# Half-batch maxima and a split mask in the first layer of a two-layer transformer kernel

## The chip, the core and the metric

One core of a Trainium2 chip. A core has TensorE (matrix products, its weight loads are shown as PEld), VectorE (DVE), ScalarE (ACT), GpSimd (POOL) and SyncE (SP, which here only issues DMAs); they meet through semaphores. The metric is the time of the whole program in microseconds on the device, where lower is better. Three runs of the kernel before gave 719.17, 721.73 and 725.0 us (median 721.73).

## The reference

Four batches of 512 tokens with 128 channels go through: a feed-forward block (ternary weights, gelu), the attention that this case is about, a second such feed-forward block, a routed block of 8 experts, a linear attention and a second routed block. The attention of the first layer has 16 heads of 8 channels and two halves. The first is a causal softmax attention whose values are the normalised input; the second, the error attention, applies masked products to what the first one failed to predict:

```python
scores = jnp.einsum('bhqd,bhkd->bhqk', q, k) * scale
scores = jnp.where(causal, scores, -jnp.inf)
y_ar = jnp.einsum('bhqk,bhkd->bhqd', jax.nn.softmax(scores, axis=-1), v)
e = v[:, :, 1:, :] - y_ar[:, :, :-1, :]
qa = -jax.nn.leaky_relu(-q2 * scale, negative_slope=0.02)
ka = jax.nn.sigmoid(k2 * scale * 0.02)
ma = jnp.einsum('bhqd,bhkd->bhqk', qa, ka)
ma = jnp.where(jnp.tril(jnp.ones((t - 1, t - 1), dtype=bool)), ma, 0.0)
y_ma = jnp.einsum('bhqk,bhkd->bhqd', ma, e)
```

## The kernel before

Tokens lie in 4 tiles of 128, heads in 4 sets of 4. A softmax needs the largest score of every query and head before the exponentials. The kernel computes the scores twice for that: once with queries on the partitions, for the **maxima**, and once with keys on the partitions, for the exponentials; the negated maxima are an additional row of the operands of the second product, so that ScalarE's exponential needs nothing more.

**Maxima.** One unit of them is a product of a query tile with a key tile of one set (128x512, on the diagonal with a second product that adds the mask) into one of two PSUM banks (turn[1] and accum[1], in turns), and VectorE's reduction of it to 128x4 (L1059, tile sb_mpart). There are 10 units to a set and 40 to a batch. `max_scores` (L1486) issues the products on TensorE, `maxima` (L1055) the reductions. After all 40, VectorE takes the largest over the tiles (`max_of_tiles`, L1063), TensorE turns the result around into turn[1] (`max_turn`, L1500), ScalarE copies it to SBUF (`max_t`, L788, tile sb_qs), and two small DMAs to a pair of sets put it into the operands (`max_row`, L398). The operands of the maxima come from DRAM, one set at a time (`next_max_set`, L390: 5 DMAs, issued when the products of the set two before are done).

**Before the attention** there is one `before_attention(b)` per batch on every engine: the feed-forward block's output product, the hidden product of the next batch, the turns and the projections of batch b-1 (`project`). Projections are split in a high and a low part and stored in DRAM (`keep_softmax`, `keep_features` on SP: 6 DMAs of 256 KB each for a batch). All 40 units of batch 0 are done here: 12 in `before_attention(2)`, 12 in `before_attention(3)` and 16 behind it. They can't start before the operands of batch 0 have been to DRAM and back.

**The attention of a batch** is a loop of 20 units of exponentials (5 to a set). In unit u TensorE issues the scores of unit u+2, the first of two maxima units of the next batch, the products with the values (`answers`, in the second, fourth and fifth unit of a set only), at the second unit of a set the turn of the answers of the set before, and the second maxima unit. ScalarE takes a unit's exponential (L812); TensorE's scores of unit u+2 wait for the exponential of unit u. At the first unit of a set ScalarE also copies the answers of the set before out of PSUM (L803). Batch 3 has no next batch, so its loop has no maxima. The operands of the exponentials are two sets deep; SP loads the set two further on when the scores of a set are through, behind the maxima's set in its queue.

**The error attention** of the batch follows. For each of 4 key tiles TensorE makes two products of 128x1024 (`ma_scores`, pair[0] and pair[1]), VectorE masks both to SBUF (L1132, tile sb_work) and masks a 128x128 state (L1137), and TensorE multiplies with the errors (`ma_answers`). The errors are GpSimd's (`errors`, L615: L624 and L625), the last of them for the last set of heads, and TensorE waits for them before the first product.

Each engine executes its own list in the order in which the Python code issues it; there is no planner. A wait thus holds back everything that stands behind it on its engine.

## Time and profile before

| | |
|---|---|
| runs | 719.17, 721.73, 725.0 us |
| profiled execution | 721.84 us, of which the span is 720.0 us |
| TensorE busy | 511.9 us (71%) |
| VectorE busy | 365.3 us (51%) |
| ScalarE busy | 196.8 us (27%) |
| GpSimd busy | 182.3 us (25%) |
| mean granted TensorE clock | 0.863 of 2.4 GHz |
| attention of the four batches | from 128.5 to 364 us |

The page's chain that ended last is by share: PE 47%, DVE 18%, POOL 11%, issue 8%, DMA 6%, ACT 5%, SP's queue 5%. Busy times are averages over stages that have different limits, so what counts is read stage by stage.

### The profile page before, as it was taken

What the parts mean: (1) busy time and instruction counts of PE and PEld (TensorE: products, weight loads), DVE (VectorE), ACT (ScalarE), POOL (GpSimd) and SP (SyncE); (2) the same over time, 40 slices, a digit from 0 to 9 for tenths busy, and PEclk for the clock granted to TensorE, in tenths of its full rate; (3) what the DMA queues carried; (4) which work ended last, traced back from release to release, by engine and by line L of the source; (5) the groups of instructions that cost most, each with busy time, mean ns of one, the idle gap of its engine ahead of it and who ended that gap; (6) DMA issues with size and microseconds to landing.
All of it is one profiled execution on the core that took longest, in us unless ns stands there. A gap on an engine that the chain in (4) does not pass through costs nothing.

```text
span 720.0 us, 9924 instructions
## 1 busy us (share of the span) xinstructions
PE 511.9 (71%) x3706; PEld 329.5 (46%) x3706; DVE 365.3 (51%) x950; ACT 196.8 (27%) x278; POOL 182.3 (25%) x208
## 2 busy tenths in 40 slices
PE   1755784799899889998878529914778888735930
PEld 1624432344634544453467517802445655524930
DVE  4444745367676856760535431224969677430211
ACT  1342231453245144336234302102223111101200
POOL 8550436001010110111012560045322022031035
PEclk9987887699999999999989958965899999655975
DMA  8434668732442253142070012114743530001213
GB/s 282 185 116 148 210 212 248 177 103 64 92 133 78 79 131 104 53 90 82 1 234 1 30 39 57 45 32 132 203 142 79 160 97 16 1 15 51 60 40 98
DMA packets 61471, 74.16 MB, mean 103 GB/s; under 512 B 6772, under 2 KB 38128, under 8 KB 61168
## 3 DMA queue, kind: packets, MB, share of 16 engines
q1 hardware_dynamic: 59376, 69.34, 33.3%
q0 software_dynamic: 2048, 4.20, 2.0%
q8 instruction: 29, 0.48, 0.3%
q14 instruction: 18, 0.15, 0.1%
HBM read 42.97 MB, written 30.41 MB: 102 GB/s over the span
## 4 chain that ended last, share of the span: by engine, by line
PE 47%; DVE 18%; POOL 11%; issue 8%; DMA 6%; ACT 5%; SPq 5%; POOLq 0%; DVEq 0%; ACTq 0%
PE ps_accum L1378 21%; PE ps_pair L1378 16%; PE ps_turn L1378 5%; POOL xe_scr L574 4%; DMA sb_ring<-sb_qs 3%; SPq L358 2%; POOL sb_rstd L558 2%; PE ps_turn L1386 2%; DVE sb_work L1132 2%; POOL sb_work L720 2%; DVE sb_work L1270 1%; DVE sb_mpart L1059 1%; DVE sb_values L969 1%; DVE sb_stats L960 1%; SPq L366 1%
## 5 line engine op out<-in xcount | busy, mean ns | idle before, releaser
L812 ACT ACTIVATE sb_work<-ps_pair 128x1024 f32<-128x1024 f32 x80 | 80.3, 1026 | 51.0 <-PE ps_pair L1378 50.2
L1059 DVE TENSOR_REDUCE sb_mpart<-ps_turn 128x4 f32<-128x512 f32 x80 | 55.0, 687 | 46.6 <-PE ps_turn L1378 46.5
L1378 PE MATMUL ps_pair<-sb_ring,sb_xsets 128*128 128x512 f32 x160 | 64.5, 480 | 15.6 <-DMA sb_ring<-sb_qs 10.1
L1059 DVE TENSOR_REDUCE sb_mpart<-ps_accum 128x4 f32<-128x512 f32 x80 | 55.0, 688 | 20.9 <-PE ps_accum L1378 20.2
L1378 PE MATMUL ps_accum<-sb_work,sb_v_aug 128*32 128x128 f32 (+3 forms) x768 | 58.6, 400 | 0.3 <-ACT sb_work L812 0.3
L1378 PE MATMUL ps_turn<-sb_ring,sb_m_sets 128*128 128x512 f32 x80 | 40.5, 506 | 20.7 <-DMA sb_m_sets<-q_scr 11.0
L1378 PE MATMUL ps_accum<-sb_ring,sb_m_sets 128*128 128x512 f32 x80 | 42.0, 525 | 3.9 <-DVE sb_mpart L1059 3.7
L1378 PEld LDWEIGHTS ps_pair<-sb_ring,sb_xsets 128*128 128x128 f32 x160 | 30.7, 199 | 26.6 <-issue 14.5
L556 POOL TENSOR_SCALAR sb_ve<-sb_mv 128x4 f32<-128x4 f32 x24 | 5.6, 235 | 144.4 <-DVE sb_mv L963 144.0
L624 POOL TENSOR_TENSOR sb_e_pad<-sb_v_next,sb_y_ar 128x128 f32<-128x128 f32 x16 | 7.3, 458 | 127.2 <-DVE sb_y_ar L1102 127.2
L1270 DVE TENSOR_TENSOR sb_work<-ps_pair,sb_cst 128x1024 f32<-128x1024 f32 x32 | 37.5, 1215 | 2.2 <-PE ps_pair L1378 2.2
L1132 DVE TENSOR_TENSOR sb_work<-ps_pair,sb_cst 128x1024 f32<-128x1024 f32 x32 | 37.7, 1218 | 1.1 <-PE ps_pair L1378 0.4
L1378 PE MATMUL ps_pair<-sb_y_tmp,sb_mw 128*128 128x256 f32 x128 | 34.9, 421 | 1.9 <-ACT sb_y_tmp L862 1.9
L1386 PE MATMUL ps_turn<-sb_cst,sb_values 128*128 128x128 f32 x48 | 10.3, 354 | 34.1 <-DVE sb_values L969 29.7
L574 POOL DMA_INDIRECT xe_scr<-sb_values,sb_slot_all x16 | 15.9, 997 | 73.3 <-DVE sb_slot_all L1040 69.7
L1378 PE MATMUL ps_pair<-sb_xs,sb_w1r 128*128 128x512 f32 x64 | 23.7, 496 | 13.7 <-DVE sb_xs L979 7.1
L1378 PE MATMUL ps_accum<-sb_mw,sb_work 128*128 128x128 f32 x256 | 31.3, 276 | 2.3 <-issue 2.3
L1378 PEld LDWEIGHTS ps_accum<-sb_mw,sb_work 128*128 128x128 f32 x256 | 30.0, 192 | 2.7 <-issue 2.6
L1378 PEld LDWEIGHTS ps_turn<-sb_ring,sb_m_sets 128*128 128x128 f32 x80 | 16.1, 201 | 30.7 <-DVE sb_mpart L1059 12.6
L1217 DVE COPY sb_e_pad<-ps_accum 128x256 f32<-128x256 f32 x16 | 6.8, 425 | 45.4 <-PE ps_accum L1378 45.4
L1378 PE MATMUL ps_pair<-sb_ring,sb_ka_stk 128*128 128x512 f32 x64 | 23.9, 483 | 7.9 <-DVE sb_work L1270 6.5
L1378 PEld LDWEIGHTS ps_pair<-sb_y_tmp,sb_mw 128*128 128x128 f32 x128 | 25.8, 212 | 7.0 <-ACT sb_y_tmp L862 3.5
(242 smaller groups left out, 1007.7 us busy)
## 6 DMA issues: line engine op xcount, KB each, us to landing
sb_m_sets<-q_scr SPq DMA_DIRECT2D x16, 256.0 KB
sb_xsets<-k_scr SPq DMA_DIRECT2D x16, 256.0 KB
sb_ka_stk<-mk_scr SPq DMA_DIRECT2D x4, 1024.0 KB
sb_mw<-in_mw SPq DMA_DIRECT2D x16, 256.0 KB, 5.2
sb_ka_stk<-mk_scr SPq DMA_DIRECT2D x8, 512.0 KB
q_scr<-sb_qs SPq DMA_DIRECT2D x12, 256.0 KB, 3.0
k_scr<-sb_ks SPq DMA_DIRECT2D x12, 256.0 KB, 3.8
sb_ring<-k_scr SPq DMA_DIRECT2D x64, 48.0 KB
```

Source lines behind the costliest of these rows:

```text
L358: sp.dma_start(ring[VW * hl:VW * hl + 3 * HD, i, hl].bitcast(F32), head_rows(q_scr, b, HL * hs + hl, 3 * HD)).then_inc(done, 16)
L366: sp.dma_start(ring[VW * hl:VW * hl + 3 * HD, 2 + i, hl].bitcast(F32), head_rows(k_scr, b, HL * hs + hl, 3 * HD)).then_inc(done, 16)
L558: pool.tensor_tensor(rstd[i][:], ve[i][:], const("minus_half"), ALU.pow).then_inc(s["rstd"], 1)
L574: pool.indirect_dma_start(xe_scr, bass.IndirectOffsetOnAxis(ap=places[:, t:t + 1], axis=0), rows_out[:, t, :], None).then_inc(s["scattered ...
L624: pool.tensor_tensor(dst, value, answer, ALU.subtract).then_inc(s["err_pad"], 1)
L720: pool.indirect_dma_start(y_last[:, b, t, :], None, ye_scr, bass.IndirectOffsetOnAxis(ap=slot_all[:, i:i + 1], axis=0)).then_inc(last_gath ...
L812: act.activation(banks[:, 2 * i:2 * i + 2], pair[u % 2][:], ACT.Exp, scale=SCALE).then_inc(s["exp_done"], 1)
L1059: dve.tensor_reduce(mpart[:, m // NPAIR, m % NPAIR, :], max_banks[m % 2][:].rearrange("p (h k) -> p h k", h=HL), AX.X, ALU.max).then_inc(s ...
L1132: dve.tensor_tensor(work[:, n % 4].rearrange("p a (h q) -> p (a h) q", h=HL), pair[n % 2][:].rearrange("p a (h q) -> p (a h) q", h=HL), bc ...
L1270: dve.tensor_tensor(work[:, n % 4].rearrange("p a (h q) -> p (a h) q", h=HL), pair[n % 2][:].rearrange("p a (h q) -> p (a h) q", h=HL), bc ...
L1378: return pe.matmul(dst, lhsT, rhs, start=start, stop=stop, skip_group_check=True)
L1386: last = pe.transpose(tile(dst, t), src[:, t, :], ident)
```

## The change

Two things change. The maxima of a batch are made in two halves (two sets, 20 units, each) with a turn of their own, and all of them come half a batch later. Before the attention only the first half of batch 0 is made, 12 units of it in `before_attention(3)` and 8 behind. The second half of batch 0 is made in the first five units of its own attention, four maxima units in each. From there on a set of maxima (10 units) goes with each set of exponentials: the loop of batch b makes the maxima's set that is three sets ahead, so that the first five units of batch 3 have maxima too. The turns of the halves now lie inside the loop, at the first unit of the second and of the fourth set. And of the two masks of each key tile of the error attention, VectorE keeps the first; the second is a copy by ScalarE and a select in place by GpSimd.

```diff
+def max_units(b, u):
+    hs, i = u // NG_X, u % NG_X
+    if b == 0 and hs == 0:
+        return HALF + 4 * i, HALF + 4 * i + 2, HALF + 4 * i + 4
+    first = NPAIR * (NS * b + NS - 1 + hs)
+    if first >= UNITS:
+        return UNITS, UNITS, UNITS
+    at = (0, 0, 3, 5, 8, 10) if hs % 2 else (0, 2, 4, 6, 8, 10)
+    return first + at[i], first + (at[i] + at[i + 1]) // 2, first + at[i + 1]
+
+
+def max_turn_in(b, u):
+    if u == NG_X:
+        return 2 * b + 1
+    if u == 3 * NG_X and b + 1 < B:
+        return 2 * b + 2
+    return None
 
 
 def build(nc, x_in, bias_cols, w_attn_t, w_k2_t, w_proj_t, b_proj, w1_t, w2_t, b2,
@@ -213,7 +234,7 @@
...
             keep_softmax(2)
+            next_max_set(0)
             keep_features(2)
+            next_max_set(1)
             keep_softmax(3)
+            keep_features(3)
             hold(sp, s["ffn_h"], NF * B)
...
-            keep_features(3)
...
-            next_max_set(0, 2)
             hold(sp, s["max_t_evac"], 1)
...
-            next_max_set(0, 3)
-            for kept in ("mq_kept", "mk_kept"):
+            for kept in ("q_kept", "k_kept", "mq_kept", "mk_kept"):
                 hold(sp, s[kept], 48 * B)
...
             for b in range(B):
+                if b == 0:
+                    next_max_set(2)
                 load_state(b)
...
                 for hs in range(NS):
-                    if b + 1 < B:
-                        next_max_set(b + 1, hs)
+                    if NS * b + NS - 1 + hs < B * NS:
+                        next_max_set(NS * b + NS - 1 + hs)
                     hold(sp, s["st_mm"], NX * b + NG_X * (hs + 1))
                     if hs + 2 < NS:
                         load_exp_set(b, hs + 2)
+                        hold(sp, s["max_t_evac"], 2 * b + 2)
                         max_row(b, hs + 2)
                     elif b + 1 < B:
                         load_exp_set(b + 1, hs + 2 - NS)
-                if b + 1 < B:
-                    hold(sp, s["max_t_evac"], b + 2)
-                    for hs in range(2):
-                        max_row(b + 1, hs)
+                        hold(sp, s["max_t_evac"], 2 * b + 3)
+                        max_row(b + 1, hs + 2 - NS)
...
+            def zero_from(b, t):
+
+                block = work[:, (2 * t + 1) % 4].rearrange("p a (h q) -> p (a h) q", h=HL)
+                pool.wait_ge(s["ma_copied"], NT * b + t + 1)
+                pool.affine_select(block, block, [[0, 2 * HL], [1, P]], ALU.is_ge, 0.0, base=-1,
+                                   channel_multiplier=-1).then_inc(s["ma_zeroed"], 1)
+
...
                 for hs in range(NS - 1):
                     errors(b, hs)
+                zero_from(b, 0)
+                errors(b, NS - 1)
+                for t in range(1, NT):
+                    zero_from(b, t)
                 if b + 1 < B:
                     values(b + 1)
-                errors(b, NS - 1)
...
+                act.copy(mT[q % 2], turn[1][0:H // 2, :]).then_inc(s["max_t_evac"], 1)
...
                         answers_out(b, hs - 1)
+                    if max_turn_in(b, u) is not None:
+                        max_t(max_turn_in(b, u))
                 answers_out(b, NS - 1)
-                if b + 1 < B:
-                    max_t(b + 1)
+                for t in range(NT):
+                    act.wait_ge(s["ma_mm"], 2 * NT * b + 2 * t + 2)
+                    if t >= 2:
+                        act.wait_ge(s["ym_mm"], NT * b + t - 1)
+                    act.copy(work[:, (2 * t + 1) % 4], pair[1][:]).then_inc(s["ma_copied"], 1)
...
             def attention(b):
...
+                for u in range(NX):
+                    hs, i = u // NG_X, u % NG_X
+                    first, _, last = max_units(b, u)
+                    maxima(first, last)
+                    if b and u == 1:
                         moments(norm_first(B + b - 1), x[b - 1], (b - 1) % 2)
-                    maxima(b + 1, 4, 6)
-                    if b:
+                    if b and u == 2:
                         normalise(norm_first(B + b - 1), x[b - 1], xn_third[b - 1], (b - 1) % 2)
-                    for hs in range(NS):
-                        maxima(b + 1, at[hs], at[hs + 1])
-                        if hs < NS - 1:
-                            answers_divide(b, hs)
-                    max_of_tiles(b + 1)
-                else:
-                    norm(norm_first(B + b - 1), x[b - 1], xn_third[b - 1])
-                    for hs in range(NS - 1):
-                        answers_divide(b, hs)
+                    if u + 1 < NX and max_turn_in(b, u + 1) is not None:
+                        max_of_tiles(max_turn_in(b, u + 1))
+                    if hs and i == 1:
...
-                for n in range(2 * NT):
+                for t in range(NT):
+                    n = 2 * t
                     dve.wait_ge(s["ma_mm"], 2 * NT * b + n + 1)
                     if n >= 4:
                         dve.wait_ge(s["ym_mm"], NT * b + (n - 4) // 2 + 1)
                     dve.tensor_tensor(work[:, n % 4].rearrange("p a (h q) -> p (a h) q", h=HL),
-                                      pair[n % 2][:].rearrange("p a (h q) -> p (a h) q", h=HL),
+                                      pair[0][:].rearrange("p a (h q) -> p (a h) q", h=HL),
                                       bc(const("key_before"), 2 * HL), ALU.mult).then_inc(s["ma_masked"], 1)
-                    if n % 2 == 1 and n // 2 < NT - 1:
-                        dve.wait_ge(s["kv_mm"], (NT - 1) * b + n // 2 + 1)
-                        dve.tensor_tensor(kv[:, n // 2, :], turn[0][:, 0:D], const("same_head"), ALU.mult).then_inc(s["kv_evac"], 1)
...
-                m = 3 * NT * (b - 2)
-                output(b, (lambda i: max_scores(0, m + i, m + i + 1)) if b >= 2 else None)
-                if b + 1 < B:
-                    hidden(b + 1, (lambda i: max_scores(0, m + 4 + i, m + 5 + i)) if b >= 2 else None)
+                last = b == B - 1
+                output(b, (lambda i: max_scores(i, i + 1)) if last else None)
+                if last:
+                    max_scores(4, 8)
                 else:
-                    max_scores(0, m + 4, m + 8)
+                    hidden(b + 1)
                 if b >= 2:
                     turn_keys(b - 2)
...
-                if b >= 2:
-                    max_scores(0, m + 8, m + 12)
+                if last:
+                    max_scores(8, 12)
...
+                    q, j = n // HALF, n % HALF
+                    if n % NPAIR == 0:
+                        pe.wait_ge(s[f"mset{hs % 2}"], 80 * (n // NPAIR // 2 + 1))
+                    if j >= 2:
+                        pe.wait_ge(s["smax_red"], (HALF + NT) * q + j - 1)
+                    elif j == 0 and q:
+                        pe.wait_ge(s["max_t_evac"], q)
...
+            def max_turn(q):
+                half = q % 2
+                pe.wait_ge(s["smax_red"], (HALF + NT) * (q + 1))
...
-                    if n >= 2:
-                        pe.wait_ge(s["ma_masked"], 2 * NT * b + n - 1)
+                    if t:
+                        pe.wait_ge((s["ma_masked"], s["ma_copied"])[pr], NT * b + t)
...
-                pe.wait_ge(s["ma_masked"], 2 * NT * b + 2 * t + 2)
+                pe.wait_ge(s["ma_masked"], NT * b + t + 1)
+                pe.wait_ge(s["ma_zeroed"], NT * b + t + 1)
...
                     if u + 2 < NX:
                         scores(b, u + 2)
-                    if ahead:
-                        max_scores(b + 1, 2 * u, 2 * u + 1)
+                    first, middle, last = max_units(b, u)
+                    max_scores(first, middle)
                     for kt in range(NT):
                         if (DIAGONAL[kt] + NT - kt - 1) // 2 == i:
                             answers(b, hs, kt)
                     if hs and i == 1:
                         turn_answers(b, hs - 1)
-                    if ahead:
-                        max_scores(b + 1, 2 * u + 1, 2 * u + 2)
+                    if max_turn_in(b, u) is not None:
+                        max_turn(max_turn_in(b, u))
+                    max_scores(middle, last)
 
                 pe.wait_ge(s["exp_done"], NX * (b + 1))
                 pe.wait_ge(s["state_in"], 112 * b + 112)
                 ma_scores(b, 0)
                 turn_answers(b, NS - 1)
-                if ahead:
...
                 if ahead:
-                    pe.wait_ge(s["max_t_evac"], b + 2)
+                    pe.wait_ge(s["smax_red"], (HALF + NT) * (2 * b + 3) + NPAIR)
```

How this moves instructions, at three places. The first is ScalarE's list in the attention of batch 0 at the start of the fourth set (ACTIVATE is the exponential, COPY the answers, CAST the turned maxima). Before:

```order
L812 ACTIVATE sb_work<-ps_pair1 128x1024 [waits s_pv_mm,s_st_mm]
L803 COPY sb_y_tmp0<-ps_accum0 128x512 [waits s_y_t,s_pv_mm]
L812 ACTIVATE sb_work<-ps_pair0 128x1024 [waits s_pv_mm,s_st_mm]
L812 ACTIVATE sb_work<-ps_pair1 128x1024 [waits s_pv_mm,s_st_mm]
L812 ACTIVATE sb_work<-ps_pair0 128x1024 [waits s_pv_mm,s_st_mm]
```

and with the change:

```order
L838 ACTIVATE sb_work<-ps_pair1 128x1024 [waits s_pv_mm,s_st_mm]
L829 COPY sb_y_tmp0<-ps_accum0 128x512 [waits s_y_t,s_pv_mm]
L822 CAST sb_qs<-ps_turn1 8x512 [waits s_xset1,s_xset0,s_max_t]
L838 ACTIVATE sb_work<-ps_pair0 128x1024 [waits s_pv_mm,s_st_mm]
L838 ACTIVATE sb_work<-ps_pair1 128x1024 [waits s_pv_mm,s_st_mm]
L838 ACTIVATE sb_work<-ps_pair0 128x1024 [waits s_pv_mm,s_st_mm]
```

The CAST stands now between two exponentials; before it stood behind the last COPY of the batch, outside the loop.

The second is GpSimd's list at the end of the attention of batch 0 (the two TENSOR_TENSOR are the errors of a set, COPY the values of the next batch). Before:

```order
L624 TENSOR_TENSOR sb_e_pad<-sb_v_next,sb_y_ar 128x4x4x8 [waits s_y_norm]
L625 TENSOR_TENSOR sb_v_next<-sb_v_next,sb_y_ar 128x4x32
L612 COPY sb_v_aug<-sb_values_1 128x64x8 [waits s_v_in,s_pv_mm]
L624 TENSOR_TENSOR sb_e_pad<-sb_v_next,sb_y_ar 128x4x4x8 [waits s_y_norm]
L625 TENSOR_TENSOR sb_v_next<-sb_v_next,sb_y_ar 128x4x32
L556 TENSOR_SCALAR sb_ve_0<-sb_mv_0 128x4 [waits s_moments]
```

and with the change:

```order
L640 TENSOR_TENSOR sb_e_pad<-sb_v_next,sb_y_ar 128x4x4x8 [waits s_y_norm]
L641 TENSOR_TENSOR sb_v_next<-sb_v_next,sb_y_ar 128x4x32
L647 AFFINE_SELECT sb_work<-sb_work 128x1024 [waits s_ma_copied]
L640 TENSOR_TENSOR sb_e_pad<-sb_v_next,sb_y_ar 128x4x4x8 [waits s_y_norm]
L641 TENSOR_TENSOR sb_v_next<-sb_v_next,sb_y_ar 128x4x32
L647 AFFINE_SELECT sb_work<-sb_work 128x1024 [waits s_ma_copied] x3
L628 COPY sb_v_aug<-sb_values_1 128x64x8 [waits s_v_in,s_pv_mm]
```

A select stands ahead of the errors of the last set, three behind them, and the values of the next batch behind all.

The third is SP's list before the attention, from batch 2's features on (mq_scr, mk_scr) over batch 3's stores to the operands of the exponentials (sb_xsets). Before:

```order
L352 DMA mq_scr<-sb_feat 16x8x512 [waits s_ma_lo]
L352 DMA mq_scr<-sb_feat 16x8x512 x2
L352 DMA mk_scr<-sb_feat 16x8x512 [waits s_ma_lo]
L352 DMA mk_scr<-sb_feat 16x8x512 x2
L352 DMA q_scr<-sb_qs 16x8x512 [waits s_split_lo]
L352 DMA q_scr<-sb_qs 16x8x512 x2
L352 DMA k_scr<-sb_ks 16x8x512 [waits s_split_lo]
L352 DMA k_scr<-sb_ks 16x8x512 x2
L358 DMA sb_ring<-q_scr 24x512 [waits s_ffn_h]
L358 DMA sb_ring<-q_scr 24x512 x3
L360 DMA sb_xsets<-k_scr 128x512
L358 DMA sb_ring<-q_scr 24x512 x4
```

and with the change, from batch 2's features on:

```order
L373 DMA mq_scr<-sb_feat 16x8x512 [waits s_ma_lo]
L373 DMA mq_scr<-sb_feat 16x8x512 x2
L373 DMA mk_scr<-sb_feat 16x8x512 [waits s_ma_lo]
L373 DMA mk_scr<-sb_feat 16x8x512 x2
L387 DMA sb_ring<-k_scr 24x512 [waits s_smax_mm]
L387 DMA sb_ring<-k_scr 24x512 x3
L389 DMA sb_m_sets<-q_scr 128x512
L373 DMA q_scr<-sb_qs 16x8x512 [waits s_split_lo]
L373 DMA q_scr<-sb_qs 16x8x512 x2
L373 DMA k_scr<-sb_ks 16x8x512 [waits s_split_lo]
L373 DMA k_scr<-sb_ks 16x8x512 x2
L373 DMA mq_scr<-sb_feat 16x8x512 [waits s_ma_lo]
L373 DMA mq_scr<-sb_feat 16x8x512 x2
```

A set of maxima with its wait (s_smax_mm) now stands ahead of the stores of batch 3.

## Rows read from the trace of the kernel before

**Rows 1.** Stretches from the span's start; busy time and count by engine, clock, DMA.

```profile
48.00:59.00 11.00, 0.07 (x1) 0.07 (x1) 0.79 (x2) 1.78 (x4) 4.89 (x4) 0.68 0.64 196
...
195.00:257.00 62.00, 56.37 (x430) 29.57 (x428) 43.18 (x78) 23.43 (x27) 6.64 (x12) 1.00 0.39 101
```

**Rows 2.** Timeline, TensorE before the attention: start, duration, instruction, idle before and releaser.

```profile
58.93 0.80 PE L1378 MATMUL ps_turn<-sb_ring,sb_m_sets 128*128 128x512 f32 x1 [11.02 <-DMA sb_m_sets<-q_scr]
...
71.87 1.98 PE L1378 MATMUL ps_pair<-sb_xnT,sb_wqk 128*128 128x512 f32 x4 [0.68 <-ACT sb_xnT L734]
...
78.09 1.05 PE L1378 MATMUL ps_accum<-sb_w,sb_h_too 128*128 128x128 f32 x8
...
91.75 3.78 PE L1378 MATMUL ps_pair<-sb_xnT,sb_wqk 128*128 128x512 f32 x4 [0.68 <-ACT sb_xnT L734]
...
104.72 1.98 PE L1378 MATMUL ps_pair<-sb_xnT,sb_wqk 128*128 128x512 f32 x4
```

**Rows 3.** Timeline, the queue of SP and what ends beside it, 108 to 129.

```profile
108.84 1.81 SPq L352 DMA_DIRECT2D q_scr<-sb_qs  x3
...
112.25 0.68 DVE L1059 TENSOR_REDUCE sb_mpart<-ps_accum 128x4 f32<-128x512 f32 x1
...
125.41 1.36 SPq L400 DMA_DIRECT2D sb_ring<-sb_qs  x2
...
128.49 0.76 PE L1378 MATMUL ps_pair<-sb_ring,sb_xsets 128*128 128x512 f32 x1 [7.78 <-DMA sb_ring<-sb_qs]
```

**Rows 4.** Timeline, the turn of the maxima: last reduction and ScalarE's copy.

```profile
118.65 0.69 DVE L1059 TENSOR_REDUCE sb_mpart<-ps_accum 128x4 f32<-128x512 f32 x1 [0.23 <-PE ps_accum L1378]
...
120.75 0.57 ACT L796 CAST sb_qs<-ps_turn 16x512 fp32r<-16x512 f32 x1 [7.24 <-PE ps_turn L1503]
```

**Rows 5.** Timeline, batch 1, border between two sets of heads.

```profile
207.51 1.95 ACT L812 ACTIVATE sb_work<-ps_pair 128x1024 f32<-128x1024 f32 x2
...
207.67 0.69 DVE L1059 TENSOR_REDUCE sb_mpart<-ps_accum 128x4 f32<-128x512 f32 x1 [0.76 <-PE ps_accum L1378]
...
208.85 0.63 PE L1378 MATMUL ps_pair<-sb_ring,sb_xsets 128*128 128x512 f32 x2
```

**Rows 6.** Timeline, VectorE's reciprocals: one per set, batches 1 and 3.

```profile
211.92 0.26 DVE L1100 RECIPROCAL sb_rcp<-ps_turn 128x16 f32<-128x16 f32 x1 [0.89 <-PE ps_turn L1538]
...
223.15 0.26 DVE L1100 RECIPROCAL sb_rcp<-ps_turn 128x16 f32<-128x16 f32 x1 [0.89 <-PE ps_turn L1538]
...
338.24 0.26 DVE L1100 RECIPROCAL sb_rcp<-ps_turn 128x16 f32<-128x16 f32 x1 [7.97 <-PE ps_turn L1538]
...
346.03 0.26 DVE L1100 RECIPROCAL sb_rcp<-ps_turn 128x16 f32<-128x16 f32 x1 [7.20 <-PE ps_turn L1538]
```

**Rows 7.** Timeline, SP's queue in batch 0.

```profile
132.28 7.68 SPq L388 DMA_DIRECT2D sb_values<-v_scr  x1
...
149.04 0.60 SPq L400 DMA_DIRECT2D sb_ring<-sb_qs  x1
```

**Rows 8.** Timeline, batch 3, first border between sets.

```profile
325.55 0.59 ACT L803 COPY sb_y_tmp<-ps_accum 128x512 f32<-128x512 f32 x1 [1.02 <-PE ps_accum L1378]
...
330.78 0.49 PE L1378 MATMUL ps_pair<-sb_ring,sb_xsets 128*128 128x512 f32 x1 [0.44 <-DMA sb_ring<-sb_qs]
```

**Rows 9.** Groups by line and form: the masks, and GpSimd's elementwise instructions.

```profile
L1132 DVE TENSOR_TENSOR sb_work<-ps_pair,sb_cst 128x1024 f32<-128x1024 f32 x32 | 37.7, 1218 | 1.1 <-PE ps_pair L1378 0.4
...
L612 POOL COPY sb_v_aug<-sb_values 128x512 f32<-128x512 f32 x4 | 2.4, 612 | 16.8 <-PE ps_accum L1378 10.0 <-DMA sb_values<-v_scr 6.8
...
L683 POOL TENSOR_TENSOR sb_x<-sb_x,sb_rows 128x512 f32<-128x512 f32 x4 | 5.1, 1272 | 3.3 <-DVE sb_values L969 3.2
...
L642 POOL TENSOR_SCALAR sb_rows<-sb_rows 128x128 f32<-128x128 f32 x1 | 1.0, 1013 | 2.4 <-DMA sb_l1wp<-in_l_wp 2.4
```

**Rows 10.** Timeline, TensorE takes up the error attention of batch 0.

```profile
179.99 0.46 PE L1378 MATMUL ps_turn<-sb_v_next,sb_ka_tok 128*128 128x128 f32 x2 [1.06 <-POOL sb_v_next L625]
```

**Rows 11.** Waits of TensorE, 197 to 241: us in total, times, longest.

```profile
PE ps_turn L1378 <- DVE sb_mpart L1059: 1.0, 2, 0.5
```

115 lines of the change are left out of this document (53 added, 62 removed).

## The prediction

> **What bounds the kernel now.** I read the busy time by stretch first, to see which stage has idle TensorE time; then TensorE's timeline before the attention, for what it waits for; then SP's queue, because it ends that stage; then the loop of the attention at a border of two sets, where the new turns go; and the groups of masks and of GpSimd's instructions for the second part of the change.
>
> Before the attention TensorE stands still from 48 to 59 (0.07 us busy) [rows 1]: the first maxima product starts at 58.93 after 11.02 us of waiting for batch 0's operands to come back from DRAM [rows 2]. From there projections of batches 1, 2 and 3 start at 71.87, 91.75 and 104.72 [rows 2]. Behind the last, SP is the path: stores of batch 3 from 108.84, the row of maxima at 125.41, first scores at 128.49 [rows 3]. In the loop TensorE is the bound: its waits for reductions are 1.0 us of 44 us [rows 11], and a set takes 223.15 - 211.92 = 11.2 us with ten maxima units against 346.03 - 338.24 = 7.8 us without [rows 6]. One maxima unit so costs (11.2 - 7.8) / 10 = 0.34 us of the path there. The error attention is VectorE's: 8 masks of 1.22 us per batch [rows 9].
>
> **Start of the attention: 13.3 us earlier.** The stall goes, since before_attention(2) has no maxima left. From 58.93 to 71.87 are 12.9 us with 8 maxima units; without them 12.9 - 8 x 0.34 = 10.2, and these now start at 47.9: projection 1 at 58.1. From there to projection 2 were 19.9 us; the four units between them and the output product at 78.09 go, so that this product starts right behind the projection's three products, some 3.1 us after their start (the first two take 1.98), instead of 6.2 [rows 2]: projection 2 at 74.9. The next interval keeps its maxima and its 13.0 us: projection 3 at 87.9, 16.8 us earlier. What is late next is SP: the stores of batch 3 started 4.1 us after the projection, but now a set of maxima with a wait for the 20th unit stands ahead. Its counterpart in place (the second unit after the projection) was reduced at 112.25, 7.5 us after it [rows 3]. That delays the chain by 3.4 us, so 16.8 - 3.4 = 13.4; the DMAs in the chain are otherwise the same, one set's load merely changes place. Bounds: -10 if saturated DMA engines delay the stores by one more wait, -18 if TensorE runs these stretches at the full clock and SP's list drains faster. I take -13.4.
>
> **The maxima moved into loops: +8.8 us.** Ten more units lie in batch 0's first five exponentials, and ten in batch 3's. Batch 0: 10 x 0.34 = 3.4, and part of them at the lower clock with which that loop starts: 4.5. Batch 3: here I follow the end instead. Its first border is set by the copy at 325.55 and ends with the scores at 330.78 that wait for a DMA [rows 8]. With 3.4 us more ahead, the last reduction falls at about 329.3; the turn chain below puts the next exponentials at 332.0, three of them follow, and the scores start at 335.1: +4.3. SP's list gives the same, as it now waits for the last maxima before it loads the set.
>
> **The turns: +17.4 us.** This is the term that decides. Before, the turn lay behind the loop, beside other work. Now the chain stands between two exponentials: last reduction, reduction over the tiles, four transposes, ScalarE's copy, and only then the exponential that TensorE's next scores need. Its length is in the trace: reduction at 118.65, copy at 120.75 for 0.57, so the next exponential starts 2.7 us after the last reduction starts [rows 4]. At a border in batch 1 the reduction starts at 207.67 and the exponential had started at 207.51 already, the scores that need it at 208.85 [rows 5]. Now: exponential at 207.67 + 2.7 = 210.4, over at 211.4, scores at 211.4 instead of 208.85, 2.55 us later. TensorE has nothing else in that unit: the two maxima units that stood there (0.68 us) have gone to later units of the set and are still to be done. The 0.3 us wait for a DMA some units later is absorbed. 2.55 + 0.68 - 0.3 = 2.9 us a turn. There are two turns in each of batches 0 to 2 (batch 3's is in the term above): 6 x 2.9 = 17.4. From both sides: 0.6 us (the transposes alone, if the rest hides) to 3.2.
>
> **SP in batch 0: +2 us.** The set ahead of the error attention's operands now waits for the 30th unit, in the third unit of the loop. Behind it stands the load that held the queue 7.68 us [rows 7], and behind that the exponentials' set that was complete after 149.04. I estimate this set some 30 us after the loop's start, about when the loop, with its extra maxima and its turn, comes to it: 0 to 5, taken 2.
>
> **The error attention: -2 us.** VectorE's list falls from two masks a tile to one: 4 x 1.22 less per batch, 19.5 us of VectorE in all. But the second half now passes ScalarE (two exponentials of that size take 1.95 us [rows 5]) and then GpSimd before TensorE may use it. No row shows a select. Below: the one-input COPY of 128x512 takes 612 ns, so 128x1024 some 1.1 us; above: the two-input form of 128x512 takes 1272 ns, so 2.5 us; farther, TENSOR_SCALAR takes 1.0 us for only 128 columns [rows 9], which would be 7 us. I take 1.5 us, between the first two and nearer to the one-input row, as a select reads one tensor. TensorE started behind the errors at 179.99 [rows 10]; one select stands ahead of these now, so it starts 1.5 us later. Then a tile takes about 2.2 us instead of 2.6: 3 x 0.4 are won, and 0.7 more at the end, where a second mask of 1.22 fell away. That is -0.5 a batch. At 1.1 us it is -1.3, at 2.5 us select follows select, and it is +2.5. So -2, with -5 and +10.
>
> The page "GPSIMD Engine Reference" of the Trainium skill (section 7) puts bodies of compare and select at 1.03 to 2.03 cycles for an element. With its 1.2 GHz that would be an estimate of 0.9 to 1.7 us for 1024, and the term -6 to +1. Its section 4.1 advises against elementwise work there but for one-input forms; here the COPY row agrees.
>
> **Sum.** -13.4 + 4.5 + 4.3 + 17.4 + 2 - 2 = +12.8, on the profiled execution's 721.84: 734.6 us. That execution stands 0.1 above the median of 721.73. I predict **734 us**. About 1% (7 us) is what a measurement of this kernel tells from no change.
>
> **Rivals.**
> 1. *The turn is covered; faster.* If the engines absorb it (TensorE gets ahead elsewhere, for instance since fewer maxima lie next to ScalarE's copy of the answers), a turn costs its 0.6 us of transposes: 6 x 2.3 = 13.8 less, and with DVE waits of 1.8 us a batch gone (rows 11 has 1.0 of them) 5 less: 734 - 19 = 715. It decides below 1 us a turn. For it: each engine's share in the loop leaves ScalarE free over half of the time. Against: the scores need exactly the exponential behind the turn, and no row shows a spare 2.5 us. 0.11.
> 2. *The start gains all that it can.* Projections at the full clock and DMAs never late would bring the loop's start forward by 24 us (the 11.0 stall, 12 units' waits before projection 2 and 3): 734 - 10 = 724, no change. Against: the stores' chain of 16.6 us behind projection 3 stays. Together with mixtures of small terms: 0.17.
> 3. *The select is slow.* At 2.35 us or more GpSimd is the bound of the error attention: 734 + 10 = 744. At 7 us it would be far more (+65). 0.14, of which 0.02 for the last.
> 4. *The clock falls.* Granted clock was 0.68 over the stretch with the 11 us pause, 1.00 over 195 to 257 with pauses of about 1 us [rows 1]. Idle times of 2.5 us lie between. If each turn cost the engine the full clock for half of the set behind it, 5.6 us of work take twice as long, and six turns add 6 x 5.6 = 34: 768. 0.06. The page "TensorE: Matmul & The Clock Gate" of the Trainium skill (Part 1) says that the lower clock is the default and recent activity lifts it; the two stretches agree with that (0.68 and 1.00), and neither tells what 2.5 us do.
>
> **Numbers.** The forecast has 0.52. Range 719 to 748: the forecast's own is 726 to 743 (start -10 to -18, turns 2.4 to 3.2, select 1.1 to 2); it is widened to rivals 2 and 3 without the 7 us case, and leaves out most of 1 and 4. Slower by over 1%: 0.52 + 0.14 + 0.06 less 0.02 for the forecast's lower edge, 0.70. Within 1%: 0.17 and half of that edge, 0.18. Faster by over 1%: 0.11 and the other half, 0.12.
>
> **What would show it.** First maxima product about 15 us after the second output product and no pause of 11 us; the first exponential scores at 115 instead of 128.5. In the loop the CAST between two exponentials, with TensorE idle about 2.5 us before the scores behind it, 7 times. A set of ten maxima with a turn at about 14 us instead of 11.2. The select at 1 to 2.5 us; error attention from the first product to the last at or a little below 15 us. Batch 0's loop longer by some 12 us, batches 1 and 2 by 6, batch 3 by 4. The prediction fails if a turn shows less than 1 us of idle TensorE, or if the start comes before 108 or after 120.

## The result

The changed kernel takes 759.25 us (median of 4 runs, 754.39 to 762.43), the kernel before beside it 721.23 us (median of 4 runs, 719.17 to 725.0). The ratio is 1.0515, with a 95% interval of 1.0443 to 1.0587: slower, as forecast, but by 38 us instead of 13, and outside the range of 719 to 748. The profiled execution, the longest of the four, has a span of 760.6 us against 720.0, so 40.6 us have to be found in the trace.

**The start** came as forecast. TensorE's timeline of the changed kernel has the projections of batches 1, 2 and 3 and then the first scores of the attention (start, duration, instruction, idle before and what ended it):

```profile
57.20 3.42 PE L1407 MATMUL ps_pair<-sb_xnT,sb_wqk 128*128 128x512 f32 x4 [0.68 <-ACT sb_xnT L760]
...
74.54 3.78 PE L1407 MATMUL ps_pair<-sb_xnT,sb_wqk 128*128 128x512 f32 x4 [0.68 <-ACT sb_xnT L760]
...
88.10 1.98 PE L1407 MATMUL ps_pair<-sb_xnT,sb_wqk 128*128 128x512 f32 x4 [0.21 <-ACT sb_xnT L760]
...
115.53 0.77 PE L1407 MATMUL ps_pair<-sb_ring,sb_xsets 128*128 128x512 f32 x1 [17.74 <-DMA sb_ring<-sb_qs]
```

Against [rows 2, 3] the loop starts at 115.53 instead of 128.49: 12.96 us won. All that is lost comes behind. To find it, the attention is cut at ScalarE's copies of the answers (one per set of heads) and at its last copy in the error attention; the first set of batch 0 is counted from the loop's first scores. The stretches of the kernel before that matter, in the view of busy time by stretch (length, then busy time and count of PE, PEld, DVE, ACT, POOL, then granted clock, DMA share, GB/s): the second and the fourth set of batch 1, its error attention, the first set of batch 3.

```profile
207.03:218.25 11.22, 10.68 (x65) 5.11 (x65) 7.27 (x12) 5.50 (x6) 0.87 (x2) 1.00 0.29 83
...
229.65:239.37 9.72, 9.48 (x60) 4.41 (x60) 6.92 (x12) 4.48 (x5) 0.87 (x2) 1.00 0.34 96
239.37:253.86 14.49, 12.72 (x171) 9.00 (x171) 11.87 (x19) 1.16 (x2) 1.48 (x3) 1.00 0.22 66
...
315.54:325.55 10.01, 8.81 (x60) 4.07 (x59) 3.75 (x14) 6.51 (x8) 2.55 (x3) 1.00 0.92 204
```

The same view of the changed kernel: the second set of batch 0; the second, third and fourth set of batch 1 and its error attention; the fourth set of batch 2; the first and second set of batch 3.

```profile
136.62:155.34 18.72, 13.49 (x70) 5.87 (x70) 8.12 (x17) 6.06 (x8) 0.87 (x2) 0.91 0.56 143
...
211.86:225.82 13.96, 11.71 (x69) 5.14 (x69) 7.52 (x16) 6.06 (x7) 0.87 (x2) 1.00 0.21 66
225.82:241.55 15.73, 13.36 (x65) 6.16 (x65) 7.19 (x12) 5.50 (x6) 0.86 (x2) 0.78 0.22 60
241.55:255.50 13.95, 10.52 (x64) 4.44 (x64) 7.52 (x16) 5.03 (x6) 0.86 (x2) 1.00 0.21 66
255.50:272.13 16.63, 13.20 (x167) 10.10 (x167) 7.02 (x10) 4.64 (x5) 5.77 (x7) 0.90 0.20 58
...
311.88:327.42 15.54, 12.13 (x64) 4.71 (x64) 7.53 (x16) 5.03 (x6) 0.87 (x2) 0.89 0.20 60
...
344.04:358.80 14.76, 12.44 (x72) 5.96 (x71) 9.39 (x23) 6.74 (x8) 2.54 (x3) 1.00 0.65 144
358.80:370.67 11.87, 9.72 (x57) 4.00 (x57) 1.68 (x7) 5.95 (x8) 0.87 (x2) 0.86 0.23 63
```

Two things are to be seen. A set with a turn is longer even where the clock stands at 1.00 (13.96 against 11.22, 13.95 against 9.72). And of stretches with the same work some have a lower clock and are some 1.6 us longer: the fourth set is 13.95 in batch 1 and 15.54 in batch 2. Set by set the differences to the kernel before are:

| | set 1 | set 2 | set 3 | set 4 | error attention | sum |
|---|---|---|---|---|---|---|
| batch 0 | +5.3 | +7.7 | -0.1 | +4.2 | +0.7 | +17.8 |
| batch 1 | 0.0 | +2.7 | +4.3 | +4.2 | +2.1 | +13.5 |
| batch 2 | 0.0 | +2.5 | -0.2 | +5.8 | +2.1 | +10.2 |
| batch 3 | +4.8 | +3.4 | 0.0 | 0.0 | +0.5 | +8.6 |

That is 50.1 us, less the 13.0 of the start: 37.1. The remaining 3.5 us (360.7 us against 357.2 from the last copy to the end) lie in code that the change doesn't touch. The profiles of the eleven experiments below, all with the same code there, have 355.6 to 364.4 us for it, so 3.5 us lie within its spread. Stages are compared below for that reason, beside the medians.

**A turn** is the chain that was forecast. Batch 1, border to the fourth set, all engines: last reduction, reduction over the tiles, transposes, ScalarE's copy, exponential, scores.

```profile
242.18 0.69 DVE L1090 TENSOR_REDUCE sb_mpart<-ps_accum 128x4 f32<-128x512 f32 x1 [1.12 <-PE ps_accum L1407]
...
243.40 0.60 PE L1537 MATMUL ps_turn<-sb_cst,sb_mneg 128*8 128x128 f32 x4 [0.57 <-DVE sb_mneg L1100]
244.03 0.57 ACT L822 CAST sb_qs<-ps_turn 8x512 fp32r<-8x512 f32 x1 [1.89 <-PE ps_turn L1537]
244.52 3.08 ACT L838 ACTIVATE sb_work<-ps_pair 128x1024 f32<-128x1024 f32 x3
245.58 0.73 PE L1407 MATMUL ps_pair<-sb_ring,sb_xsets 128*128 128x512 f32 x2 [1.58 <-ACT sb_work L838]
...
251.42 0.51 PE L1407 MATMUL ps_accum<-sb_ring,sb_m_sets 128*128 128x512 f32 x1 [0.72 <-DVE sb_mpart L1090]
...
254.16 0.49 PE L1407 MATMUL ps_turn<-sb_ring,sb_m_sets 128*128 128x512 f32 x1 [0.56 <-DVE sb_mpart L1090]
```

TensorE waits 0.57 us for the tiles and 1.58 for the exponential. The last two rows are new: ten maxima units are left for four units of a set, two of which have no scores beside them in the fourth set, and TensorE waits for VectorE's reductions (1.3 us in all).

**The error attention** starts later. GpSimd and TensorE, batch 1:

```profile
258.14 1.10 POOL L647 TENSOR_SCALAR_AFFINE_SELECT sb_work<-sb_work 128x1024 f32<-128x1024 f32 x1 [6.56 <-ACT sb_work L848]
259.22 0.45 POOL L640 TENSOR_TENSOR sb_e_pad<-sb_v_next,sb_y_ar 128x128 f32<-128x128 f32 x1
259.63 0.45 POOL L641 TENSOR_TENSOR sb_v_next<-sb_v_next,sb_y_ar 128x128 f32<-128x128 f32 x1
260.18 0.46 PE L1407 MATMUL ps_turn<-sb_v_next,sb_ka_tok 128*128 128x128 f32 x2 [2.72 <-POOL sb_v_next L641]
260.40 1.17 PE L1407 MATMUL ps_pair<-sb_qa_pad,sb_ka_stk 128*128 128x512 f32 x4
261.49 1.94 PE L1407 MATMUL ps_accum<-sb_work,sb_e_pad 128*32 128x128 f32 x32
...
265.65 1.08 PE L1407 MATMUL ps_accum<-sb_work,sb_e_pad 128*32 128x128 f32 x32
266.66 0.49 PE L1407 MATMUL ps_turn<-sb_v_next,sb_ka_tok 128*128 128x128 f32 x2
266.90 1.17 PE L1407 MATMUL ps_pair<-sb_qa_pad,sb_ka_stk 128*128 128x512 f32 x4
267.91 0.38 PE L1407 MATMUL ps_accum<-sb_qaf,sb_kv 128*128 128x128 f32 x2
268.22 1.08 PE L1407 MATMUL ps_accum<-sb_work,sb_e_pad 128*32 128x128 f32 x32
...
270.43 1.08 PE L1407 MATMUL ps_accum<-sb_work,sb_e_pad 128*32 128x128 f32 x32 [0.71 <-POOL sb_work L647]
```

The select takes 1.10 us, at the cheap end of what I had allowed. But it begins just as the answers that the errors need are there, so the errors wait its full length, and TensorE pauses for 2.72 us instead of 1.06 [rows 10]. (The other 0.6 us of that difference are the turn's transposes, which filled a part of this wait before.) Behind the pause the same 32 products take 1.94 us, and a tile later 1.08. From 265.65 to 268.22 TensorE works without a gap: a tile is 2.57 us of its own work. In the kernel before the same tile, and VectorE's list beside it (two masks and the masked state), are these:

```profile
247.08 2.36 DVE L1132 TENSOR_TENSOR sb_work<-ps_pair,sb_cst 128x1024 f32<-128x1024 f32 x2
247.75 1.08 PE L1378 MATMUL ps_accum<-sb_work,sb_e_pad 128*32 128x128 f32 x32
249.35 0.28 DVE L1137 TENSOR_TENSOR sb_kv<-ps_turn,sb_cst 128x128 f32<-128x128 f32 x1
250.37 1.08 PE L1378 MATMUL ps_accum<-sb_work,sb_e_pad 128*32 128x128 f32 x32
```

VectorE has 2.36 + 0.28 = 2.64 us of work in a tile, and the tile took 2.62.

### The profile page after: what moved, and what is told of

It reads as the page before. It is cut to its first block, busy times and chain, and to the rows that moved or that the text cites. A ratio compares the mean times of both kernels' runs of the same rounds, so it can differ in the third digit from the quotient of the medians.

```text
span 760.6 us, 10026 instructions
## 1 busy us (share of the span) xinstructions
PE 529.1 (70%) x3722; PEld 336.0 (44%) x3722; DVE 348.8 (46%) x950; ACT 215.4 (28%) x298; POOL 199.3 (26%) x224
## 4 chain that ended last, share of the span: by engine, by line
PE 46%; DVE 17%; POOL 11%; issue 8%; ACT 7%; SPq 6%; DMA 4%; POOLq 0%; DVEq 0%; ACTq 0%
PE ps_accum L1407 21%; PE ps_pair L1407 15%; PE ps_turn L1407 6%; DVE sb_mpart L1090 3%; POOL xe_scr L590 2%; POOL sb_rstd L574 2%; PE ps_turn L1415 2%; DMA sb_ring<-sb_qs 2%; POOL sb_work L746 2%; DVE sb_work L1299 2%; POOL sb_work L647 2%; DVE sb_stats L991 1%; ACT sb_work L838 1%; SPq L379 1%; SPq L373 1%
## 5 line engine op out<-in xcount | busy, mean ns | idle before, releaser
L1407 PE MATMUL ps_pair<-sb_ring,sb_xsets 128*128 128x512 f32 x160 | 68.1, 501 | 40.0 <-DMA sb_ring<-sb_qs 24.2
L1407 PE MATMUL ps_accum<-sb_work,sb_v_aug 128*32 128x128 f32 (+3 forms) x768 | 62.1, 419 | 0.3 <-ACT sb_work L838 0.3
L1407 PE MATMUL ps_turn<-sb_ring,sb_m_sets 128*128 128x512 f32 x80 | 41.0, 512 | 10.6 <-DVE sb_mpart L1090 10.3
L1299 DVE TENSOR_TENSOR sb_work<-ps_pair,sb_cst 128x1024 f32<-128x1024 f32 x32 | 37.5, 1214 | 2.5 <-PE ps_pair L1407 2.4
L1407 PE MATMUL ps_pair<-sb_ring,sb_ka_stk 128*128 128x512 f32 x64 | 24.5, 492 | 10.3 <-DVE sb_work L1299 8.9
L647 POOL TENSOR_SCALAR_AFFINE_SELECT sb_work<-sb_work 128x1024 f32<-128x1024 f32 x16 | 17.5, 1095 | 49.0 <-ACT sb_work L848 49.0
L760 ACT COPY sb_xnT<-ps_turn 128x512 f32<-128x512 f32 x16 | 9.3, 584 | 73.0 <-PE ps_turn L1415 73.0
```

The lines of the kernel that those rows point to most:

```text
L647: pool.affine_select(block, block, [[0, 2 * HL], [1, P]], ALU.is_ge, 0.0, base=-1, channel_multiplier=-1).then_inc(s["ma_zeroed"], 1)
L760: act.copy(dst, bank[:]).then_inc(s["x2_ready"], 1)
L1299: dve.tensor_tensor(work[:, n % 4].rearrange("p a (h q) -> p (a h) q", h=HL), pair[n % 2][:].rearrange("p a (h q) -> p (a h) q", h=HL), bc ...
L1407: return pe.matmul(dst, lhsT, rhs, start=start, stop=stop, skip_group_check=True)
```

## The experiments

Theory A, formed from these rows: three delays in the changed kernel sit in the order of instructions and not in the work (the first select ahead of the errors, ScalarE's copy ahead of the exponential, a queue of DMAs), and each lets TensorE pause long enough that the lower clock often follows. Its main rival C: the two parts of the change disturb each other. "Ratio" is to the kernel before, with its 95% interval. The kernel before was timed anew with each group of experiments: its median is 723.55 us for e1 to e4, 722.15 for e5 to e8 and 724.06 for e9 to e11. The changed kernel was timed only in the group of the result, where the kernel before had 721.23, so a difference to its 759.25 us can be off by some 3 us.

**e1, masks alone.** The kernel before with the ScalarE copy and GpSimd select (here only GpSimd's order is shown):

```
+                zero_from(b, 0)
+                errors(b, NS - 1)
+                for t in range(1, NT):
+                    zero_from(b, t)
```

> The kernel before with only the second part of the change: the second mask of each key tile as a ScalarE copy and a GpSimd select, maxima as before. Theory A (the first select, 1.1 us long, stands ahead of the last errors, and TensorE's longer pause costs it the full clock for some microseconds): about +5 us against the kernel before, from 5.4 us more in the four error attentions of the changed kernel's trace; 726. Rival B (the step of the prediction, VectorE's lighter list wins a little in each tile): -2 us; 719. Rival C (the two parts disturb each other, and the masks are behind most of the missing 25 us): over +15 us.

734.55 us, ratio 1.0147 (1.0061 to 1.0233). The error attentions are 16.6, 15.1, 16.6 and 17.4 us against 16.0, 14.5, 14.5 and 14.1: +6.7 us, near theory A's +5. The median rose by 11 us, and these stages do not show the rest (in the profiled execution the untouched code behind the attention took 364.4 us, the most of all). B is out: this part costs time. TensorE's pause is 2.1 us in the first three, where the turn's transposes fill 0.6 us of it, and 2.73 in the last.

**e2, maxima alone.** The changed kernel with VectorE's two masks and without `zero_from`.

> The changed kernel with both masks on VectorE again: the half-batch maxima alone. Theory A: the start 13 us earlier, the loops 45 us longer (moved maxima 10, seven turns 25, late operands 10), so about +32 us against the kernel before; 753. Rival C (the masks are behind most of the missing 25 us): +13 to +20 us; 734 to 741. The stretches of the loops should be as in the changed kernel, the error attentions 14.5 us as before.

754.37 us, ratio 1.0415 (1.0334 to 1.0496). +30.8 here and +11.0 in e1 make 41.8, where both together gave 38: they add up within the spread. C is out. The error attentions are 14.5, 14.5, 15.8 and 14.1.

**e3, errors first.**

```
-                zero_from(b, 0)
                 errors(b, NS - 1)
-                for t in range(1, NT):
+                for t in range(NT):
```

> The changed kernel with the errors of the last set ahead of all four selects on GpSimd, nothing else. Theory A (the first select holds the errors back): TensorE's wait for the errors falls from 2.7 to about 1.6 us, 1.1 us less in each of four error attentions, and up to 1 us more in each if the lower clock behind this wait goes too: 4 to 8 us less than the changed kernel, 751 to 755. Rival D (TensorE then waits for the select instead, the chain of copy and select is what counts): no change, 757 to 761.

749.64 us, ratio 1.0357 (1.026 to 1.0455): 9.6 us less than the changed kernel, more than D allows, and more than A's 4 to 8. GpSimd and TensorE in batch 1:

```profile
253.38 0.45 POOL L640 TENSOR_TENSOR sb_e_pad<-sb_v_next,sb_y_ar 128x128 f32<-128x128 f32 x1 [6.57 <-DVE sb_y_ar L1134]
253.79 0.46 POOL L641 TENSOR_TENSOR sb_v_next<-sb_v_next,sb_y_ar 128x128 f32<-128x128 f32 x1
254.19 1.10 POOL L647 TENSOR_SCALAR_AFFINE_SELECT sb_work<-sb_work 128x1024 f32<-128x1024 f32 x1
254.34 0.46 PE L1406 MATMUL ps_turn<-sb_v_next,sb_ka_tok 128*128 128x128 f32 x2 [1.66 <-POOL sb_v_next L641]
...
255.73 1.08 PE L1406 MATMUL ps_accum<-sb_work,sb_e_pad 128*32 128x128 f32 x32
```

The pause is 1.66, the first products take 1.08, and nobody waits for the first select: its product comes 0.45 us after its end. The stages are 14.09, 14.07, 14.09 and 15.26 us, together 6.9 us less than in the changed kernel; the last one had the lower clock in it (0.89).

**e7, masks alone, errors first.** e1 with the order of e3.

> The split masks alone on the kernel before, as e1, but with the errors of the last set ahead of all selects. Theory A (the split as such wins a little per tile, as the prediction said, and the placement of the first select lost it): error attentions of 14.1 us against 14.5 (15.95 in batch 0) before and 15.1 to 17.4 in e1: 2 to 3 us less than the kernel before, ratio 0.995 to 0.998. Rival B2 (the chain of copy and select is too long even so): still 3 us or more slower than the kernel before.

723.69 us, ratio 1.0018 (0.9983 to 1.0053). The stages are 14.07, 14.08, 14.10 and 13.69, the last three 0.4 us below those of the kernel before, and the first 1.9 us, because that stage had the lower clock in the kernel before (0.89). That is what A says of the stages. Its ratio for the whole, 0.995 to 0.998, lies just below the interval: no gain in the whole time is shown. B2 (3 us or more) is just inside the interval, but the stages speak against it, and the 11 us of e1 are gone by the order of two lines on GpSimd.

**e11, filler.** The changed kernel with work for TensorE in its pause:

```
                 turn_answers(b, NS - 1)
+                for _ in range(4):
+                    turn_tiles(accum[0], y_tmp[1].rearrange("p (t q) -> p t q", t=NT))
                 pe.wait_ge(s["ka_tok"], b + 1)
```

> The changed kernel with 16 more transposes of 128x128 on TensorE into a bank that is free then, between the turn of the last answers and the wait for the errors, in each error attention; their result is overwritten. They fill most of the 2.7 us wait with work and change no order or dependence. Theory A (the products behind this wait run at the lower clock because of the pause): the products behind it take 1.08 instead of 1.94 us for 32, and an error attention of 16.6 us becomes 15.0; 4 to 6 us less than the changed kernel, 754. Rival I (they are slow for another reason, ScalarE's and GpSimd's traffic for instance): they stay slow, 16.6 us and 759.

752.78 us, ratio 1.039 (1.0332 to 1.0447): 6.5 us less than the changed kernel with more work in it. Batch 1:

```profile
257.06 1.91 PE L1415 MATMUL ps_accum<-sb_cst,sb_y_tmp 128*128 128x128 f32 x16
257.92 1.10 POOL L647 TENSOR_SCALAR_AFFINE_SELECT sb_work<-sb_work 128x1024 f32<-128x1024 f32 x1 [6.58 <-ACT sb_work L848]
...
259.94 0.46 PE L1407 MATMUL ps_turn<-sb_v_next,sb_ka_tok 128*128 128x128 f32 x2 [0.97 <-POOL sb_v_next L641]
```

The chain is the same (the select still ahead of the errors, TensorE's products with the errors 2.0 us after the select's start), only the pause is filled. The first three stages go from 16.61, 16.63 and 16.62 to 15.07, 15.06 and 15.07, and their granted clock from 0.90 to 1.00; the fourth had 1.00 in both and stays at 14.59. So some 1.55 us of each of the three was the lower clock behind the pause, in one execution each; I is out.

**e4, ScalarE's copy one exponential later.**

```
-                    if max_turn_in(b, u) is not None:
-                        max_t(max_turn_in(b, u))
+                    if u and max_turn_in(b, u - 1) is not None:
+                        max_t(max_turn_in(b, u - 1))
```

(Not shown: in the second unit of the second and fourth set all of TensorE's maxima products go behind the products with the values.)

> The changed kernel with ScalarE's copy of the turned maxima one exponential later, so that the exponential which TensorE's next scores need no longer stands behind it; the first maxima product of the next half goes behind the products with the values in its unit. Theory A (the turn costs by its chain between two exponentials): TensorE's 1.58 us wait behind each of seven turns goes, 11 us less than the changed kernel, up to 16 where a lower clock behind it goes too; 743 to 748. Rival E (the wait only moves: the maxima of the next half need the bank that the copy frees, and VectorE's reductions, now packed into fewer units, hold TensorE): 3 us less at most, 756 to 759.

743.98 us, ratio 1.0302 (1.0221 to 1.0383): 15.3 us less than the changed kernel. The sets with a turn fall from 13.96, 13.95, 13.95 and 15.54 to 12.78, 12.79, 12.81 and 12.79, that of batch 3 from 11.87 to 8.40, and none of them is at the lower clock. TensorE behind the turn in batch 1 waits for the tiles and the reductions only, and the wait for the exponential is gone:

```profile
234.08 0.60 PE L1537 MATMUL ps_turn<-sb_cst,sb_mneg 128*8 128x128 f32 x4 [0.56 <-DVE sb_mneg L1100]
238.20 0.50 PE L1407 MATMUL ps_turn<-sb_ring,sb_m_sets 128*128 128x512 f32 x1 [0.56 <-DVE sb_mpart L1090]
240.93 0.50 PE L1407 MATMUL ps_accum<-sb_ring,sb_m_sets 128*128 128x512 f32 x1 [0.71 <-DVE sb_mpart L1090]
```

But the second set of batch 0 did not fall: it took 20.46 us, against 18.71 in the changed kernel. The wait for the exponential went there too, and another one grew, from 2.87 us in the changed kernel to 5.84:

```profile
132.76 7.89 SPq L409 DMA_DIRECT2D sb_values<-v_scr  x1
...
148.19 0.80 PE L1407 MATMUL ps_pair<-sb_ring,sb_xsets 128*128 128x512 f32 x1 [5.84 <-DMA sb_ring<-sb_qs]
```

**e5, maxima one unit earlier.** e4 with `(0, 3, 5, 8, 10, 10)` for `(0, 2, 4, 6, 8, 10)`.

> The later copy of the run before (e4), and besides the maxima of the first and third set of a batch end one unit earlier (three, two, three and two units behind the first four exponentials), so that VectorE's reduction over the tiles is done when TensorE comes to the turn. Theory A (of a set with a turn, 12.8 us against 11.2, TensorE's 0.57 us wait for the tiles and 0.5 us behind it are left): 6 times 0.6 to 1.0 less, 4 to 6 us less than the 744 of e4; 738 to 740. Rival F (VectorE's list is full there, it also has the moments of the batch before): the waits come back as waits for reductions, no change; 742 to 747.

745.88 us, ratio 1.0317 (1.0262 to 1.0372): no gain, rival F. The sets with a turn do fall to 12.2, but the sets ahead of them rise from 14.7 to 15.8 and from 11.1 to 12.2, where TensorE now waits for the packed reductions.

**e6, another order in SP's queue.** e4 with the values of batch 1 behind the row of maxima and the operands of the third set first.

> e4 with another order in SP's queue in batch 0: the operands of the third set of exponentials are loaded first, as soon as its buffer is free, and the values of batch 1 (which held the queue for 7.9 us) behind the row of maxima. Theory A (the wait of 5.8 us in the second set of batch 0 is the queue's order): this set falls from 20.5 to about 13 us, 7 us less than e4; 737. Rival G (the DMA engines are full there, whatever the order): the wait moves to the next set or to the error attention; 742 to 747.

745.41 us, ratio 1.0327 (1.0275 to 1.0379). No gain either: the wait in the second set of batch 0 is still 4.45 us, and the set takes 19.02. The reason is in one row: the eight microseconds did not move with the values but fell on what now stood in their place, a set of maxima.

```profile
134.05 0.38 SPq L403 DMA_DIRECT2D sb_v_next<-v_scr  x1
136.05 8.15 SPq L387 DMA_DIRECT2D sb_ring<-k_scr  x4
```

Ahead of both stand the seven DMAs of `load_state`, 2 MB together.

**e10, the error attention's operands first.** e4 with one line moved.

```
+                load_state(b)
                 if b == 0:
                     next_max_set(2)
-                load_state(b)
```

> e4 with only the loads of the error attention's operands of batch 0 ahead of the maxima's set that waits for the 30th unit. Theory A: TensorE's wait of 5.8 us in the second set of batch 0 falls to 0 to 1.5 us, and this set from 20.5 to 13 to 15 us: 6 us less than e4; 738. Rival G: the wait stays at 4 us or more, or the first set becomes later by as much; 742 to 747.

736.59 us, ratio 1.0186 (1.0128 to 1.0244): 7.4 us less than e4. The second set of batch 0 is 13.15 us instead of 20.46. In SP's queue nothing is held any more; the next DMA is issued 12.4 us after the last of the seven:

```profile
113.23 0.34 SPq L403 DMA_DIRECT2D sb_v_next<-v_scr  x1
126.01 1.54 SPq L387 DMA_DIRECT2D sb_ring<-k_scr  x4
127.59 0.35 SPq L389 DMA_DIRECT2D sb_m_sets<-q_scr  x1
128.06 0.38 SPq L409 DMA_DIRECT2D sb_values<-v_scr  x1
```

G is out.

**e8, halves for batch 0 alone.** The start of the changed kernel; the second half of batch 0's maxima and one turn in its loop; then whole batches with the turn behind the loop, as before. Masks as before, queue as e6.

```
+    if b == B - 1:
+        return UNITS, UNITS, UNITS
+    if b:
+        return NM * (b + 1) + 2 * u, NM * (b + 1) + 2 * u + 1, NM * (b + 1) + 2 * u + 2
+def max_turn_in(b, u):
+    return 1 if b == 0 and u == NG_X else None
```

> Halves for batch 0 alone, masks as before: the first half ahead of the attention, the second in the first five units of its loop with one turn (copy one exponential later, queue in the order of e6), and then the maxima of batches 1 to 3 as in the kernel before, 40 units in the rest of a loop and the turn behind it; batch 3 has none. Theory A (the start gives 13 us, and what the change lost lies in the later turns, in batch 3 and in the masks): -13, +5 for the first set of batch 0, +3.4 for ten units more in the rest of its loop, +1.5 for its turn: 3 us less than the kernel before, ratio 0.996. Rival H (60 units in one loop: VectorE's reductions of 0.69 us, or the sets' loads, become the bound in batch 0): 3 to 10 us slower than the kernel before.

727.6 us, ratio 1.0064 (1.0025 to 1.0103). Batches 1 and 2 take 61.9 and 62.2 us from last copy to last copy, against 61.5 and 61.7 before, and batch 3 46.6 against 47.2, so almost nothing of the loss is left there. Batch 0 has it: 18.7 us for its second set, with a 3.67 us wait for the same DMA, and 13.7 and 13.4 for the third and fourth, where 11.4 and 9.7 stood before. The median, 5.5 us above that of the kernel before, lies in H's range, not in A's.

**e9, what the others point to.** e8 with e7's masks and, as in e10, the loads of the error attention's operands ahead of all waits of the loop in SP's queue.

> e8 (halves for batch 0 alone) with the split masks of e7 (errors ahead of all selects), and in SP's queue the loads of the error attention's operands right at the start of batch 0's loop, ahead of everything that waits there. Theory A (in e6 and e8 the instruction behind these loads held the queue for 8 us whatever it was, so it is their backlog; asked for 15 us earlier it is over before the third set is due): the second set of batch 0 falls from 18.7 to 13 us, and the four error attentions are 14.1 us: 7 us less than e8, 720; ratio to the kernel before 0.993 to 0.999. Rival G (the DMA engines are the limit in batch 0, in any order): the wait stays, 725 or more.

719.43 us, ratio 0.9941 (0.9907 to 0.9975): faster than the kernel before by 0.6%, a small step whose interval leaves out 1, and than the changed one by some 5%. The second set of batch 0 is 13.17 us and the error attentions are 14.31, 14.08, 14.08 and 13.67. So G is out here too. The third and fourth set of batch 0 stay at 13.7 and 13.4: TensorE waits 2.2 us for reductions in them, against 0.5 before, so the half of H that is about the reductions holds in small.

## Why the prediction was wrong, step by step

The direction and the mechanism of the largest cost were right. The sum was short by 25 us, 24 of them in these terms:

- **Start: -13.4 forecast, -13.0 measured.** Projections at 58.1, 74.9 and 87.9 were forecast and came at 57.2, 74.5 and 88.1, the loop at 115.5 for 115. Right, by the step that was least sure: a pause moved on to the next late thing, SP's stores.
- **Maxima in batch 0: +4.5, measured +5.3.** Right within its size.
- **Maxima and turn in batch 3: +4.3, measured +8.1.** The size failed. I had added 3.4 us to one border and let the turn vanish in waits that were there already. Ten units cost 4.8 in the first set alone (10.01 to 14.76), and the turn 3.4 in the next, of which 1.6 were the lower clock (the same set takes 10.27 at the full clock in e11); with ScalarE's copy later this set is back at 8.40, against 8.49 before.
- **Turns in batches 0 to 2: +17.4, measured about 22.** At the second set 2.9 was right (2.7 and 2.5; e4 gives back 1.2 of it and leaves 1.6 for the transposes and the wait for the tiles). At the fourth set it is 4.2, since I had read my border [rows 5] in a set with scores in every unit, and not in the fourth, where the deferred maxima have no cover: the 1.3 us of waits for reductions above. One turn in this execution also had the lower clock behind it (5.8).
- **SP's queue in batch 0: +2, measured about 5.** Here the reading failed. I had taken the 7.68 us [rows 7] for the length of that load. The time went to whichever DMA stood behind the seven (e6), so it is their backlog, and the change had put just those behind the wait for the 30th unit. One line moved wins it back (e10).
- **A late set in batch 1: 0, measured +4.3.** The set has a wait of 2.4 us for the same kind of DMA, and the lower clock (0.78):

```profile
234.79 0.79 PE L1407 MATMUL ps_pair<-sb_ring,sb_xsets 128*128 128x512 f32 x1 [2.37 <-DMA sb_ring<-sb_qs]
```

In the profiles of e2, e3, e4 and e11, which have the same order in the queue there, the same wait is 0.6 to 1.3 us, and the set takes 11.1 to 11.8. So a short wait belongs to this order, and the rest is particular to this execution; why it was longer stays open.

- **Error attention: -2, measured +5.4.** This is the step that failed most. Per batch I had 1.5 us of delay by the first select and 1.9 won in the tiles (2.2 us each instead of 2.6, and 0.7 at the end). That is -0.4, and -0.8 with a select of 1.1 us; the -0.5 and -1.3 that I wrote don't follow from these terms. The delay was 1.0. But without any delay (e7) all that is won is 0.4 us: TensorE's own work in a tile is 2.57 us, so it takes over as the bound the moment VectorE's 2.64 falls. I had called this stage VectorE's from its masks [rows 9] and had not added up TensorE's tile. And I gave the pause itself no cost: 1.0 of delay and 1.55 of clock less 0.4 are the +2.1 of batches 1 and 2.
- **Clock: rival 4, held at 0.06.** It came true in small. I had asked only whether 2.5 us of pause cost the full clock for half a set (5.6 us each); they cost it for less, 1.55 us a time, and not each time. In this execution it was three error attentions (that of batch 0 had the lower clock before, too), two turns and the late set. Against rival 1 all of it speaks: no turn was covered. Rival 2 is out with the start at 13.0 us instead of 24, and rival 3 with a select of 1.10 us instead of 2.35.

The section of "GPSIMD Engine Reference" in the Trainium skill that puts compare and select at 1.03 to 2.03 cycles an element (section 7) fits: 1095 ns for 1024 elements over 16 selects, 1.28 cycles by the page's 1.2 GHz. The estimate from the row of a one-input COPY [rows 9] had been the same 1.1 us without it. What it could not say is where in GpSimd's list that time would fall.

## What to carry to other kernels

An operation put on a lightly loaded engine costs by its place in that engine's list: e1 and e7 differ in the order of two lines, and by 11 us in their medians. When a change gives TensorE a new pause like those here (2.1 and 2.7 us, or 0.57 and 1.58 close together), allow for the lower clock behind it besides the wait, and ask what filled that pause before. Before an engine is relieved, add up the other engines' work in the same stage: here TensorE, with 2.57 us in a tile, stood less than 0.1 us behind VectorE. And a chain over several engines belongs one step behind the instruction that others wait for (e4). That it is cheapest where it happens once, e9 suggests; it was not tried alone.
